# The linear half of block-sparse attention moved from behind the softmax steps into them

## The reference, cut to what matters

```python
c_q, c_k = softmax(q, -1), softmax(k, -1)
kvb  = einsum('bhmkd,bhmke->bhmde', c_kr, vr)     # one 64x64 sum for each block m
comp = 1.0 - sel                                  # the blocks that were not picked
kv_q = einsum('bhnm,bhmde->bhnde', comp, kvb)     # what is left for query block n
num  = einsum('bhnqd,bhnde->bhnqe', c_qr, kv_q)
o_l  = num / (den[..., None] + EPS)               # den: the same with the sums of c_k
o    = o_s + proj(o_l)                            # o_s: softmax over the 6 picked blocks
```

## Time and profile before

| | |
|---|---|
| median of 3 runs | 9544.37 us (9543.76 to 9558.14) |
| the profiled execution's own time | 9540.7 us |
| its span, first to last instruction | 9538.9 us |
| mean granted clock of TensorE | 0.898 of full |
| busy: PE, DVE, ACT, POOL | 7960.4, 4952.7, 3515.8, 3224.9 us |
| passes of layer 1 | 32 |

### The profile page before, as it was taken

The page is one execution under the profiler, slowest core; times in us unless marked ns, Lnnn a source line. Parts: engine busy times, 40 slices in busy tenths (PEclk is TensorE's granted clock), DMA queues, the critical chain, the costliest instruction groups (busy, mean ns, idle before and its releaser), DMA issues.

```text
span 9538.9 us, 191259 instructions
## 1 busy us (share of the span) xinstructions
PE 7960.4 (83%) x58476; PEld 5494.8 (58%) x58476; DVE 4952.7 (52%) x11779; ACT 3515.8 (37%) x8599; POOL 3224.9 (34%) x8100
## 2 busy tenths in 40 slices
PE   8977899777997789977899778997789977899788
PEld 5655566555665556655566555665556655566555
DVE  3465544655446554465544655446554465544655
ACT  1145521445214452144421444214442145421454
POOL 2323333333332333333333243333433324333243
PEclk9988899888998889988899888998889988899788
DMA  2112121121211222111121112211122111221212
GB/s 95 62 26 39 46 84 62 29 37 47 83 62 29 37 47 82 62 32 36 50 78 62 32 35 52 76 62 34 34 54 74 62 33 35 56 71 62 38 31 60
DMA packets 828762, 497.70 MB, mean 52 GB/s; under 512 B 591312, under 2 KB 788112, under 8 KB 825424
## 3 DMA queue, kind: packets, MB, share of 16 engines
q1 hardware_dynamic: 827728, 485.16, 19.8%
HBM read 68.68 MB, written 33.55 MB: 11 GB/s over the span
## 4 chain that ended last, share of the span: by engine, by line
PE 37%; issue 32%; POOL 13%; DVE 7%; POOLq 4%; DMA 3%; ACT 2%; SPq 1%; DVEq 1%; ACTq 0%
PE PS L608 11%; POOL arena L546 9%; PE PS L668 7%; DVE arena L1194 4%; DMA arena<-arena 3%; POOL arena L531 3%; PE PS L625 3%; PE PS L648 3%; PE PS L882 2%; POOLq L540 2%; POOLq L545 2%; PE PS L691 1%; PE PS L693 1%; PE PS L804 1%; PE PS L636 1%
## 5 line engine op out<-in xcount | busy, mean ns | idle before, releaser
L951 ACT ACTIVATE arena<-PS 128x384 f32<-128x384 f32 (+5 forms) x3552 | 1461.1, 440 | 2607.1 <-PE PS L608 594.9
L546 POOL COPY arena<-arena 64x129 f32 x6144 | 1530.8, 293 | 1128.6 <-issue 827.6
L608 PE MATMUL PS<-arena 128*128 128x256 f32 x6144 | 1360.7, 380 | 46.2 <-DMA arena<-arena 45.9
L608 PEld LDWEIGHTS PS<-arena 128*128 128x128 f32 x6144 | 1156.5, 189 | 271.6 <-issue 98.5
L486 POOL TENSOR_TENSOR arena<-arena 128x512 f32<-128x512 f32 x768 | 803.7, 1069 | 1495.8 <-PE PS L608 1477.7
L1107 DVE COPY arena<-PS 64x260 f32<-64x260 f32 (+2 forms) x1272 | 634.6, 515 | 1296.3 <-PE PS L608 523.7
L793 PE MATMUL PS<-arena 64*64 64x192 f32 x8192 | 687.9, 409 | 723.5 <-POOL arena L546 485.2
L1107 DVE COPY arena<-arena 64x129 f32 x4096 | 786.4, 254 | 442.4 <-PE PS L815 217.2
L1317 DVE TENSOR_REDUCE SM<-PS 128x1 f32<-128x384 f32 x1024 | 571.1, 558 | 682.8 <-PE PS L793 366.2
L492 POOL TENSOR_TENSOR BUF<-BUF,arena 128x512 f32<-128x512 f32 x256 | 358.8, 1402 | 1673.7 <-ACT arena L987 1673.7
L1194 DVE RECIPROCAL arena<-arena 128x512 f32<-128x512 f32 x256 | 857.4, 3349 | 115.8 <-ACT arena L999 114.5
(11 more groups left out here) (102 smaller groups left out, 9926.8 us busy)
## 6 DMA issues: line engine op xcount, KB each, us to landing
arena<-arena SPq DMA_DIRECT2D x1792, 128.0 KB, 3.3
arena<-arena SPq DMA_DIRECT2D x768, 144.5 KB
BUF<-in_x SPq DMA_DIRECT2D x18, 2048.0 KB, 11.8
arena<-arena SPq DMA_DIRECT2D x2048, 16.2 KB, 3.6
out<-BUF SPq DMA_DIRECT2D x64, 512.0 KB, 2.6
arena<-in_taps SPq DMA_DIRECT2D x96, 288.0 KB, 3.6
W<-in_w SPq DMA_DIRECT2D x2, 768.0 KB, 5.9
WP<-in_wp SPq DMA_DIRECT2D x1, 512.0 KB, 5.0
```

The source lines that it names most:

```text
L546: last = pool.tensor_copy(G[p % GD][0:D, j // 3, j % 3, :], KVB[0:D, bass.ds(off, KVW)])
L608: last = nc.tensor.matmul(bank(i)[:, a * 256:(a + 1) * 256], lhsT=TW[n % 2][:, a * CH + k * P:a * CH + (k + 1) * P], rhs=src[:, k // 2:k / ...
L951: return nc.scalar.activation(o, i, ACT.Copy)
```

## The change

Four things move.

1. **Turning.** `turn_kv` goes. SP writes each group of 8 blocks to a tensor in the chip's main memory (`kv_out(j)`, 64 partitions x 8 runs of 260 bytes), and reads it back as 8 rows of 16,640 bytes on 8 neighbouring partitions (`kv_in(j)`). These 16 transfers stand within the token stage's order on SP; `kv_in(j)` waits until `kv_out(j)` has landed, and everything behind it on SP waits too.
2. **Complements.** PE sums them in iteration p = 1, after `scores(1)`, into banks 4 to 7, once all eight `kv_in` have landed. ACT and DVE copy them out before they go on with their own steps.
3. **Linear products.** `apply(p)` adds two of them to its own; DVE divides both halves at once, once for 3 steps, with one small addition more.
4. **Outputs.** `turn_probs(p)` also turns the output of step p - 7, and ACT copies it (`store_out`) behind the exponential. After the last step 7 outputs are left to be turned.

The diff, cut to its core (indents shortened):

```diff
+TRIOS = (NP + 2) // 3
+TURN_LAG = 7
...
+kv_rows = nc.dram_tensor("kv_rows", (NBLK, D, D1), F32).ap()
...
-    def turn_kv(blocks):
-        for m in blocks:
-            if m % 8 == 0:
-                sp.wait_ge(s_kvd, hd * 8 + m // 8 + 1)
-            sp.dma_start(KVM[m:m + 1, :, :], KVD[:, m, :]).then_inc(s_rel[m % 8], 16)
+    def kv_out(j):
+        sp.wait_ge(s_kvd, hd * 8 + j + 1)
+        sp.dma_start(kv_rows[8 * j:8 * j + 8].rearrange("m d e -> d m e"),
+                     KVD[:, 8 * j:8 * j + 8, :]).then_inc(s_kvo[j % 2], 16)
+    def kv_in(j):
+        sp.wait_ge(s_kvo[j % 2], hd * 64 + 16 * (j // 2 + 1))
+        sp.dma_start(FOLD[8 * j:8 * j + 8, :],
+                     kv_rows[8 * j:8 * j + 8].rearrange("m d e -> m (d e)")).then_inc(s_rel[j], 16)
...
         for j in range(max(0, 2 * gr - 2), 2 * gr if gr < 3 else 8):
+            if j >= 2:
+                kv_in(j - 2)
             k_to_upper(j)
-    q_to_upper(0)
-    q_to_upper(1)
+            if j == 7:
+                q_to_upper(0)
+                q_to_upper(1)
+            kv_out(j)
+    kv_in(6)
+    kv_in(7)
...
     def turn_probs(p):
+        x = p - TURN_LAG
         pe.wait_ge(s_p, hd * NP + p + 1)
         if p >= 2:
             pe.wait_ge(s_pt, hd * NP + p - 1)
+        if x >= 2:
+            pe.wait_ge(s_one, hd * NP + x - 1)
+        if x >= 0:
+            pe.wait_ge(s_on, hd * TRIOS + x // 3 + 1)
+            turn_out(x, 4 + p % 2, 3 * P)
         for i in range(3):
             last = nc.tensor.transpose(PS[:, 4 + p % 2, i * P:(i + 1) * P],
                                        PR[p % 2][:, i * P:(i + 1) * P], ident)
         last.then_inc(s_t, 1)
...
-    for p in range(NP + 2):
-        if p < NP:
-            scores(p)
-        if 1 <= p <= NP:
-            turn_probs(p - 1)
-        if p >= 2:
-            apply(p - 2)
-    for k in range(8):
-        pe.wait_ge(s_rel[k], (hd + 1) * 128)
-    pe.wait_ge(s_pt, (hd + 1) * NP)
-    settle(pe)
-    for r in range(5):
...
-    def linear(q):
-        if q >= 2:
-            pe.wait_ge(s_onl, hd * QUADS + q - 1)
-            settle(pe)
-        for p in range(4 * q, 4 * q + 4):
...
+    def complements():
+        for k in range(8):
+            pe.wait_ge(s_rel[k], (hd + 1) * 16)
+        pe.wait_ge(s_cmp, b + 1)
+        settle(pe)
+        for r in range(4):
+            complement(r, 0, 4 + r)
+        pe.wait_ge(s_kqa, hd * 4 + 3)
+        pe.wait_ge(s_kqd, hd * 5 + 3)
+        complement(4, 0, 6)
+        pe.wait_ge(s_kqa, hd * 4 + 2)
+        pe.wait_ge(s_kqd, hd * 5 + 2)
+    def apply(p):
+        pe.wait_ge(s_pt, hd * NP + p + 1)
+        t = p // 3
+        if p == 0:
+            pe.wait_ge(s_kqa, (hd + 1) * 4)
+            pe.wait_ge(s_kqd, (hd + 1) * 5)
+        if p % 3 == 0 and t >= 2:
+            pe.wait_ge(s_on, hd * TRIOS + t - 1)
...
+            nc.tensor.matmul(
+                PS[D * blk:D * (blk + 1), 6 + t % 2, at:at + D1],
+                lhsT=PT[p % 2][:, i * P + D * blk:i * P + D * (blk + 1)],
+                rhs=G[p % GD][:, blk, i, D:KVW], start=(i == 0), stop=(i == 2))
+    for blk in range(2):
+        n = 2 * p + blk
+        last = nc.tensor.matmul(
+            PS[D * blk:D * (blk + 1), 6 + t % 2, at + D1:at + 2 * D1],
+            lhsT=QO[hl][D:P, n * D:(n + 1) * D], rhs=KVQ[:, n, :],
+            start=True, stop=True)
+    last.then_inc(s_o, 1)
...
+    for p in range(NP + 2):
+        if p < NP:
+            scores(p)
+        if p == 1:
+            complements()
+        if 1 <= p <= NP:
+            turn_probs(p - 1)
+        if p >= 2:
+            apply(p - 2)
+    pe.wait_ge(s_on, (hd + 1) * TRIOS)
+    pe.wait_ge(s_one, (hd + 1) * NP - TURN_LAG)
+    for x in range(NP - TURN_LAG, NP):
+        k = x - (NP - TURN_LAG)
+        last = turn_out(x, 4 + k // 4, k % 4 * P)
+        if k % 4 == 3 or x == NP - 1:
+            last.then_inc(s_ot, 1)
+pe.wait_ge(s_one, (b * NH + 2 * hp + 2) * NP)
...
+    def store_out(p):
+        x = p - TURN_LAG
+        copy(QO[hl][:, x * P:(x + 1) * P], PS[:, 4 + p % 2, 3 * P:4 * P]).then_inc(s_one, 1)
+    def store_complements():
+        for r in range(4):
+            act.wait_ge(s_cq, hd * 5 + r + 1)
+            copy(KVQ[:, :, 16 * r:16 * r + 8],
+                 PS[0:D, 4 + r, :].rearrange("p (e n) -> p n e", e=8)).then_inc(s_kqa, 1)
...
+        if p == 1:
+            store_complements()
...
+        if p > TURN_LAG:
+            store_out(p - 1)
         if p + LEAD < NP:
...
-    for r in range(4):
-        act.wait_ge(s_cq, hd * 5 + r + 1)
-        copy(KVQ[:, :, 16 * r:16 * r + 8],
-             PS[0:D, r, :].rearrange("p (e n) -> p n e", e=8)).then_inc(s_kqa, 1)
-    for q in range(QUADS):
-        act.wait_ge(s_ot, hd * QUADS + q + 1)
-        copy(QO[hl][:, q * CH:(q + 1) * CH], PS[:, 4 + q % 2, :]).then_inc(s_one, 1)
+    act.wait_ge(s_ot, hd * 2 + 1)
+    left = NP - TURN_LAG
+    copy(QO[hl][:, left * P:(left + 4) * P], PS[:, 4, :]).then_inc(s_one, 4)
+    act.wait_ge(s_ot, hd * 2 + 2)
+    copy(QO[hl][:, (left + 4) * P:], PS[:, 5, 0:(TURN_LAG - 4) * P]).then_inc(s_one, TURN_LAG - 4)
...
+    vorder = Order(dve, s_dvec, hd * 2 * TRIOS, 2 * TRIOS)
+    def normalise(t):
+        n = min(3, NP - 3 * t)
+        o = PS[:, 6 + t % 2, 0:2 * n * D1].rearrange("p (j s c) -> p j s c", j=n, s=2)
+        dn = DNQ[:, 0:2 * n].rearrange("p (j s) -> p j s", j=n)
+        rn = RNQ[:, 0:2 * n].rearrange("p (j s) -> p j s", j=n)
+        dve.wait_ge(s_o, hd * NP + 3 * t + n)
+        vorder.after(nc.vector.tensor_tensor(dn.unsqueeze(3), o[:, :, :, D:D1], EPSV.unsqueeze(
+            1).unsqueeze(3).broadcast_to([P, n, 2, 1]), ALU.add))
+        vorder.after(nc.vector.reciprocal(RNQ[:, 0:2 * n], DNQ[:, 0:2 * n]))
+        on = ONA[:, 3 * t * P:(3 * t + n) * P].rearrange("p (j s c) -> p j s c", j=n, s=2)
+        nc.vector.tensor_tensor(on, o[:, :, :, 0:D], rn.unsqueeze(3).broadcast_to([P, n, 2, D]),
                                 ALU.mult).then_inc(s_on, 1)
...
-    def normalise_linear(q):
-        o = PS[:, 6 + q % 2, 0:4 * D1].rearrange("p (j c) -> p j c", j=4)
-        dve.wait_ge(s_l, hd * QUADS + q + 1)
-        vorder.after(nc.vector.tensor_scalar(DNQ.unsqueeze(2), o[:, :, D:D1], LIN_EPS, None,
-                                             ALU.add))
-        vorder.after(nc.vector.reciprocal(RNQ, DNQ))
...
+    def store_complements():
+        for r in range(5):
+            dve.wait_ge(s_cq, hd * 5 + r + 1)
+            if r < 4:
+                last = copy(KVQ[:, :, 16 * r + 8:16 * r + 16],
+                            PS[D:P, 4 + r, :].rearrange("p (e n) -> p n e", e=8))
+            else:
+                last = copy(KVQ[:, :, D:D1], PS[0:D, 6, 0:NBLK].unsqueeze(2))
+            last.then_inc(s_kqd, 1)
+        if p == 1:
+            store_complements()
...
-        if p >= 6 and p % 4 == 2:
-            normalise((p - 6) // 4)
+        if p >= 5 and p % 3 == 2:
+            normalise((p - 5) // 3)
+    for t in range((NP - 1 - 5) // 3 + 1, TRIOS):
+        normalise(t)
```

More of the change, by code:

```diff
@@ L150, in build @@
         NM = heads.take(2)
-        DNQ = heads.take(4)
-        RNQ = heads.take(4)
+        DNQ = heads.take(6)
+        RNQ = heads.take(6)
         MX8 = heads.take(8 * NH)
@@ L290, in build @@
         s_kqd = sem("kv_of_queries_by_dve")
-        s_l = sem("linear_attended")
-        s_onl = sem("linear_normalised")
+        s_kvo = [sem(f"kv_written{i}") for i in range(2)]
         s_ot = sem("outputs_turned")
@@ L731, in turn @@
                                 if p == 2 and hl == 1:
[L732 removed]
+                                    pe.wait_ge(s_one, hd * NP)
                                 sg = SG[p % 3]
@@ L797, in scores, with turn_out @@
                                 last.then_inc(s_s, 1)
+                            def turn_out(x, bank, at):
+                                return nc.tensor.transpose(PS[:, bank, at:at + P], ONA[:, x * P:(x + 1) * P], ident)
                             def turn_probs(p):
+                                x = p - TURN_LAG
                                 pe.wait_ge(s_p, hd * NP + p + 1)
@@ L806, in turn_probs, with complement @@
                                 last.then_inc(s_t, 1)
[L808 to L819, removed]
-                            for p in range(NP + 2):
-                                if p < NP:
-                                    scores(p)
-                                if 1 <= p <= NP:
-                                    turn_probs(p - 1)
-                                if p >= 2:
-                                    apply(p - 2)
-                            for k in range(8):
-                                pe.wait_ge(s_rel[k], (hd + 1) * 128)
-                            pe.wait_ge(s_pt, (hd + 1) * NP)
-                            settle(pe)
-                            for r in range(5):
+                            def complement(r, at, bank):
                                 for k in range(8):
```

(36 more changed lines are left out.)

40 lines of the change are left out of this document (7 added, 33 removed).

## The result

| | before | after |
|---|---|---|
| median of 4 runs | 9550.58 us | 9425.34 us (9415.03 to 9438.61) |
| the profiled execution, its span | 9538.9 us | 9413.1 us |
| mean granted clock of TensorE | 0.898 | 0.912 |
| busy PE, DVE, ACT, POOL | 7960.4, 4952.7, 3515.8, 3224.9 us | 7665.0, 4925.7, 3525.0, 3219.1 us |

What follows compares the result with a forecast made beforehand. POOL was taken to pace the steps, PE the tail, transfers the token stage's end. Tail -24.3, steps +2.0, head +25.3 made +3.0 us a pass, times 32 +96: 9640 us, 1.0% slower; range 9290 to 9810.

Steps and rivals of the forecast that it cites:

- the head: From SP's first spread of the last quarter to POOL's gather 4: 44.1 us against 18.8, +25.3 a pass.
- the steps: POOL's period stays 2.31 us, PE's and ACT's additions hidden; +2.0 us a pass for low-clock starts and dips.
- the tail with the clock gain: After the last apply: 25.65 us shrinks to 2.4, plus about 1 from a faster-clocked next stage; -24.3 a pass.
- The rival in which ACT or DVE takes over: In the steps ACT or DVE becomes the bound, 0.15 us on 28 steps; 9770 us, chance 0.13.
- The sign that I had named against myself: In the steps: POOL waiting for PE, ACT or DVE in most steps would show the forecast wrong.
- the sum of the transfers: In SP's queue before the complements, summed transfer times decide, six kv_in giving 15.6 us; total 31.2 us.
- 2.6 us for a `kv_in`: In the head: a read onto eight neighbouring partitions has two ways in of 25 GB/s each.
- my sign for being right: In the head: complements starting about 31 us after SP's first spread of the last quarter.
- that for being wrong: In the head: complements starting at 20 to 22 us after SP's first spread of the last quarter.
- its rival of fast reads: In the head: kv_in costs 0.74 us, the chain of landings binds at about 21; 9310 us, chance 0.22.
- `kv_out` at 1.0 us: In the head: each write to main memory taken at 1.0 us, between 0.8 and 1.6; 4.0 for kv_out.
- The single way in: In the head: all eight rows share one way in, kv_in 5.3 us, +16 a pass; 10150 us, chance 0.05.

Runs made afterwards that it cites:

- e4_turn_behind: Changed kernel, but all 32 outputs are turned after the last step in groups of four, linear products kept in the steps; 9537.7 us.
- e12_fourth_alone: Changed kernel with each read's eight rows on every fourth of 32 partitions, column constant in the same order; 9317.5 us.
- e2_out_twice: Changed kernel with every kv_out issued a second time into an unread tensor, the complements waiting for all of them; 9521.8 us.
- e1_order: Changed kernel with the last quarter reordered: transfers scores(0) needs, then all kv_out, then all kv_in, with four semaphores; 9532.2 us.
- e3_spaced: Changed kernel with each read's rows on partitions j, j+8 and so on, column constant left as it was; 9331.8 us.

## Why the prediction was wrong

A pass came out at -3.1 us where +3.0 was forecast. Of the 6.1 between, the head has -7.9, the steps up to the last apply +1.3 and the tail with the clock gain +0.5.

**The tail.** Right: 25.9 to 2.5 us, 2.4 forecast, and the token stage gained 0.4 to 0.5 us from the clock where 1.0 was estimated.

**The steps.** +2.4 and 0.9 behind the last gather, where 2.0 stood. POOL's 2.31 us stayed in 492 of 864 intervals (569 before), and e4_turn_behind shows that the transpose and ACT's copy are hidden. The rival in which ACT or DVE takes over did not occur. That the size nearly fits is in part luck: two or three steps at 3.1 us behind the complements were charged, and the first two intervals behind gather 4 are as long as before; most of the time is lost in single intervals below the full clock all over the pass. The sign that I had named against myself, POOL waiting for PE in most steps, did occur in the rows and says little, since most of these waits lie within POOL's own 0.83 us: the sign should have been the interval.

**The head.** This is the step that failed: "But the sum of the transfers decides", with 15.6 us for six `kv_in`. It put the complements at 31.2 us behind T0, and they start at 24.3, between my sign for being right (about 31) and that for being wrong (20 to 22). Two things were wrong in it.

The first is the term. 2.6 us for a `kv_in` came from 25 GB/s onto one partition, read off 16 issues in 10.26 us. But the engines were nearly idle in that stretch (share 0.14), and 0.64 us for an issue is what SP's other issues take as well (0.66 and 0.73 there): the row shows SP's pace and no limit of a partition.

```profile
3122.60:3126.60 4.00, 1.25 (x12) 0.67 (x16) 1.91 (x9) 1.01 (x4) 2.89 (x12) 0.50 0.14 25
```

That 2.6 came near the 2.0 us of reads in a row is luck. In the changed kernel, with other transfers between the reads, a read's records take 1.2 us. Its last read in windows, and then the stretch up to its landing:

```profile
3088.50:3089.50 1.00, 0.86 (x8) 0.25 (x8) 0.48 (x4) 0.00 (x0) 0.00 (x0) 0.50 0.60 141
3089.50:3092.30 2.80, 0.92 (x8) 0.34 (x9) 1.41 (x8) 1.08 (x3) 0.00 (x0) 0.50 0.01 0
```

A share of 0.60 for 1.00 us on 8 of 16 engines is 1.2 us a record. The last ends about 1.9 us before PE starts. In e12_fourth_alone the same read has 0.46, 0.9 us a record, and 0.7 us from its end to PE's start:

```profile
3064.80:3065.80 1.00, 0.84 (x8) 0.34 (x8) 0.18 (x1) 0.00 (x0) 0.00 (x0) 0.50 0.46 133
```

The second is the sum itself. What ends last is a chain, shown above for one pass. On average over 32 passes: `kv_out(5)` is issued at T0 + 6.2 and lands 5.9 us later; SP, which waited for it in front of `kv_in(5)`, issues `kv_out(7)` 2.4 us later, at 14.5; that lands after 5.4, and from the issue of `kv_in(7)` at 20.0 it is 4.3 to the complements. Of the six reads only the last is on it with its own time. The others act through the landings, because neighbouring rows slow down the transfers beside them: the 256-byte records of the old transfers take 31 ns in this stretch and the 260-byte ones of the writes 29, in e12_fourth_alone 22 and 20, and in the kernel before the former took 23. The same chain in e12_fourth_alone:

```profile
3053.24 3.73 DMA kv_rows<-arena
...
3059.77 3.81 DMA kv_rows<-arena
...
3063.59 2.87 DMA arena<-kv_rows
```

Two landings and a read are 10.4 us there and 15.4 in the changed kernel. The complements start 4.0 us earlier on average (issues that take longer give back the rest), and the kernel gains 108 us, 3.4 us a pass. That is the price of neighbouring rows, and not the 330 us between the forecast and its rival of fast reads.

`kv_out` at 1.0 us was right as time at the engines (512 records of 29 ns on 16 engines are 0.93 us), but an added one costs the path 0.5 (e2_out_twice). What follows the complements, 7.9 us and the refill (36.9 - 24.3 - 7.9 = 4.7 us), came as worked out.

**The rivals.** The fast reads were priced at 9310 with complements at 21 us. With the rows spread (e12_fourth_alone) the kernel takes 9317 with complements at 20.3: that sum was right, and so was its mechanism, the chain of landings. The changed kernel has this chain too, with longer landings in it, and lies between the rival and the forecast, at 9425, nearer to the rival. The single way in, 10150, is excluded.

## What to carry to other kernels

Add up transfers only where nothing in the queue waits for a landing. Where it does, follow the chain (issue, landing, next issue) and ask of each transfer whether it lengthens a link. A slow transfer does so for its neighbours as well: look at their landings and not only at its own. For long rows try the spacing of the partitions (here eight rows on every fourth of 32 partitions, where neighbours cost 1.1% of the kernel). Before a rate is read off a row of issues, look whether the engines were busy in it. When a wait changes its name, look at the interval before drawing a conclusion.

## What the runs showed of the hardware

- A read of 8 rows of 16,640 bytes has 8 records, one a row. With four reads in a row they took 1.9 us each onto eight neighbouring partitions (e1_order, 133 KB every 2.0 us), 1.1 onto every second or every eighth, and 0.85 onto every fourth.
- Such reads onto neighbours slow down other transfers: the median write landed in 5.2 us beside them (changed kernel) and in 3.7 when only the rows' places changed (e12_fourth_alone, e3_spaced).
- From the end of the last record to the start of the engine that waits it was 1.6 us on average with neighbouring rows (changed kernel) and 0.7 with every fourth (e12_fourth_alone).
- Every eighth partition was no better than every second (9411 and 9420), every fourth was (9345).
